# A decoder kernel whose softmax attentions mix the values over 8 or 16 columns a head instead of 128

## What is computed

```python
x = x + _L1_attn_ref(_layernorm(x), wq, wk, wv, wo)            # causal, 16 heads of 16
...
x = x + _L3_xattn_ref(_layernorm(x), ctx_1024, pos, pos, Wq, Wkv, Wout, bout)

def _L3_xattn_ref(x, ctx, ...):                                 # 32 heads of 8
    ...
    logits = jnp.einsum('bqhd,bkhd->bhqk', q, k) * scale
    w = jax.nn.softmax(logits, axis=-1)
    attn = jnp.einsum('bhqk,bkhd->bqhd', w, v)                  # the mixing of the values
    attn = attn.reshape(b, n, N_HEADS * HEAD_DIM)
    return attn @ Wout + bout
```

## Time and profile before

| | us |
|---|---|
| median of 3 runs | 2254.9 |
| lowest and highest | 2252.02, 2262.86 |
| span of the profiled execution | 2252.8 |
| TensorE matmul, weight load busy in it | 1368.1, 911.5 |
| VectorE, ScalarE, GpSimd busy in it | 1396.6, 559.6, 606.4 |

### The profile page before, as it was taken

The page is one execution under the profiler, slowest core; times in us unless marked ns, Lnnn a source line. Parts: engine busy times, 40 slices in busy tenths (PEclk is TensorE's granted clock), DMA queues, the critical chain, the costliest instruction groups (busy, mean ns, idle before and its releaser), DMA issues. The chain is left out here.

```text
span 2252.8 us, 24830 instructions
## 1 busy us (share of the span) xinstructions
PE 1368.1 (61%) x6308; PEld 911.5 (40%) x6308; DVE 1396.6 (62%) x2114; ACT 559.6 (25%) x1431; POOL 606.4 (27%) x449
## 2 busy tenths in 40 slices
PE   4525554887068943553597504798476989936760
PEld 2201123665038811111354303575244878825550
DVE  5489986333347758998875794312366767674332
ACT  1322211221016551220211001332124545502220
POOL 0046633332610005662200262133300000014335
PEclk8756665999579965656798756899687989968895
DMA  5112204986313021221000001207205310056773
GB/s 181 68 41 93 96 3 130 272 249 209 94 50 109 25 77 56 93 74 56 0 0 0 2 10 25 76 26 225 73 0 102 40 31 1 2 189 176 216 215 99
DMA packets 148450, 196.40 MB, mean 87 GB/s; under 512 B 34344, under 2 KB 109242, under 8 KB 147724
## 3 DMA queue, kind: packets, MB, share of 16 engines
q1 hardware_dynamic: 116876, 146.05, 21.8%
q0 software_dynamic: 11328, 30.95, 5.1%
q10 hardware_dynamic: 20160, 18.36, 2.4%
HBM read 153.55 MB, written 41.75 MB: 87 GB/s over the span
## 5 line engine op out<-in xcount | busy, mean ns | idle before, releaser
L141 POOL TENSOR_SCALAR rstd<-moments 128x8 f32<-128x8 f32 x12 | 2.9, 239 | 626.8 <-DVE moments L129 626.8
L442 PE MATMUL psum<-l1s_conv_out,w_ident 128*128 128x512 f32 x128 | 104.8, 965 | 107.6 <-DVE l1s_conv_out L538 107.6
L442 PE MATMUL psum<-l0s_conv_out,w_ident 128*128 128x512 f32 x128 | 103.0, 950 | 110.4 <-DVE l0s_conv_out L538 110.4
L1326 ACT ACTIVATE l3x_prob<-psum,l3x_neg_max 128x256 f32<-128x256 f32 x256 | 118.8, 469 | 107.4 <-DVE l3x_neg_max L1347 107.4
L534 DVE TENSOR_TENSOR_SCAN l1s_relu<-l1s_t_sq,l1s_xpad 128x1024 f32<-128x1024 f32 x32 | 139.7, 4365 | 5.2 <-ACT l1s_t_sq L505 5.2
L534 DVE TENSOR_TENSOR_SCAN l0s_relu<-l0s_t_sq,l0s_xpad 128x1024 f32<-128x1024 f32 x32 | 139.6, 4364 | 5.2 <-ACT l0s_t_sq L505 5.2
L1302 PE MATMUL psum<-l3x_v,l3x_probT 128*128 x1024 | 138.6, 279 | 1.1 <-DVE l3x_probT L1361 1.1
L152 PE MATMUL psum<-w_ident,h 128*128 128x128 f32 x144 | 32.4, 417 | 175.1 <-DVE h L133 175.1
L1347 DVE TENSOR_REDUCE l3x_neg_max<-psum 128x2 f32<-128x512 f32 x128 | 88.0, 690 | 67.2 <-PE psum L1267 67.2
L1302 PEld LDWEIGHTS psum<-l3x_v,l3x_probT 128*128 128x128 f32 x1024 | 127.5, 196 | 1.8 <-issue 1.8
L408 POOL TENSOR_TENSOR l1s_xpad<-l1s_du,l1s_bc 128x1024 f32<-128x1024 f32 x32 | 106.2, 3319 | 67.0 <-DVE l1s_relu L534 66.8
(11 more groups left out here) (577 smaller groups left out, 3498.1 us busy)
## 6 DMA issues: line engine op xcount, KB each, us to landing
l0f_w_in<-in_l0f_w_in SPq DMA_DIRECT2D x56, 352.0 KB
l0s_bc<-l0s_scratch SPq DMA_DIRECT2D x16, 1024.0 KB, 5.0
l1s_bc<-l1s_scratch SPq DMA_DIRECT2D x16, 1024.0 KB, 5.2
l3f_w_in<-in_l3f_w_in SPq DMA_DIRECT2D x64, 192.0 KB
l0f_w_down<-in_l0f_w_down SPq DMA_DIRECT2D x56, 176.0 KB
l2f_w_in<-in_l2f_w_in SPq DMA_DIRECT2D x24, 352.0 KB
l3f_y_rows<-h SPq DMA_DIRECT2D x16, 512.0 KB, 7.2
l3f_y_rows<-l3f_y ACTq DMA_DIRECT2D x64, 128.0 KB
```

The lines of the kernel that those rows point to most:

```text
L442: ins = nc.tensor.matmul(m.pair(2 + c)[:, cols], lhsT=m.ident[:], rhs=rhs[:, cols], start=start, stop=stop, skip_group_check=True)
L1326: ins = nc.scalar.activation(self.prob[h % self.SCORES][:, qt, 0:keys], self.bank(h % self.SCORES)[:, qt * S:qt * S + keys], ACT.Exp, bias ...
```

## The change

`mix` streams `self.hd` columns (16 in `l1a`, 8 in `l3x`) and writes as many. The stationary operand, the number and order of the instructions, the waits, the memory and its layout stay as they are.

```diff
--- before.py
+++ after.py
@@ -1297,9 +1297,9 @@
                 for qt in range(2):
                     kts = range(qt + 1) if self.causal else range(2)
                     for kt in kts:
-                        v = self.v[:, bass.ds(i * (2 * KD * 2 * P) + ((u * KD + c) * 2 + kt) * P + hh * self.hd, P)]
+                        v = self.v[:, bass.ds(i * (2 * KD * 2 * P) + ((u * KD + c) * 2 + kt) * P + hh * self.hd, self.hd)]
                         at = qt * 2 * P + hh * self.hd
-                        ins = nc.tensor.matmul(self.bank(6 + c)[:, at:at + P], lhsT=self.probT[h % 2][:, kt, qt, :],
+                        ins = nc.tensor.matmul(self.bank(6 + c)[:, at:at + self.hd], lhsT=self.probT[h % 2][:, kt, qt, :],
                                                rhs=v, start=(kt == 0), stop=(kt == kts[-1]))
                 ins.then_inc(self.mixed, 1)
```

## The result

The changed kernel takes 2469.7 us (median of 4 runs, 2464.3 to 2479.9) beside 2253.5 us for the kernel before (2248.2 to 2262.9): the ratio is 1.096, 95% interval 1.092 to 1.100. The forecast of 2479 us, slower, came out 9 us too high. The profiled execution has a span of 2478.0 us and lies 10 us above its median.

A forecast was written before the change was run, and what follows sets the result against it. TensorE was taken as the bound in `l3x`, with TensorE and VectorE both nearly full in `l1a`. Terms 64 + 156 + 4 = +224 on the 2252.8 us span gave 2477, 2479 as median; range 2405 to 2512.

The forecast's parts named there:

- The pace of a pass: L1302 in both loops: weight loads set the pace, so narrowing saves nothing; 0.111 us at high clock, 0.214 at low.
- The clock: `l1a` and `l3x`: streaming holds the clock, weight loads do not; both loops stay at 0.50 (1.2 GHz) in whole length.
- `l3x` loop: Context attention loop at the low clock throughout: 397 us where it had 241, +156; +180 with the seam unchanged.
- `l1a` loop: Causal attention loop at the low clock throughout: 156 us where it had 91.5, +64.
- the rest: Behind each loop, 16 transposes and the start of the projection at the low clock: about +2 each, +4.
- The seam of `l3x`: From mix to score: 0 to 0.1 us a unit saved at high clock; at low clock 0.15 us instead of 0.35.
- The middle of `l3x`: Waits mid-loop: 3.0 us ahead of the second trip, 2.9 for first exponentials, 1.5 for first copy; unchanged by slow clock.
- The seam of `l1a`: From mix to score: no seam, the score's load follows the mix with no rest; six passes 1.28 us.
- Only `l3x` stays low: Rival: `l1a` has more streaming left and rises in its first units; 2413 us, chance 0.10.
- The clock holds: Rival: in both loops scores and transposes alone lift the clock, only the seam is left; 0 to -12 us, chance 0.06.
- The clock goes up and down: Rival: in the loops, as in the state-space loop; half the term or less, 2300 to 2400 us, chance 0.04.
- The pace follows the columns: Rival: the mix costs next to nothing, VectorE bounds `l3x`, 50 us come off; about 2203 us, chance 0.02.

The follow-up runs named there:

- six wide units: Changed kernel, but the first six units of each trip of both loops stream 128 columns, all others 16 and 8: 2397.2 us, 1.062 of the kernel before.
- half-wide pair: Changed kernel with `l1a` at 128 columns, `l3x` matmuls alternating 128 and 8; from the first unit 2412.9 us, behind six fully wide units per trip 2245.3 us.
- half-wide behind six wide units: Changed kernel with `l1a` at 128 columns; `l3x` matmuls alternate 128 and 8 after six fully wide units per trip: 2245.3 us, 0.995 of the kernel before.

## Why the prediction was right

**The pace of a pass.** Held: 0.111 us with 16 or 8 columns at the high clock (run with six wide units), 0.214 at the low one (after). The forecast took the high one from L1602 and the routers and the low one from wide passes, and those rows carried over.

**The clock.** Held, with its place: both loops stay at 0.50 from their first unit to their last. The step "both loops begin at 0.50 and lose exactly what lifted them" was the right one, and the half-wide pair shows how much hangs on the first half of that sentence. One support of it was weak: "The one with 64 columns keeps 1.00" reads a hold from 3 us of a router. L1602 and the router with 16 columns, which fell, carried the argument.

**The Trainium skill's rule of idle gaps** ("TensorE: Matmul & The Clock Gate", section "Why this matters for your kernels": no idle gaps, and the clock stays up). In after, TensorE is busy 185.00 of 185.00 us at 0.50. The measurement decides against the rule for these loops.

**The Trainium skill's one rate for a weight load** ("TensorE: Matmul & The Clock Gate", section "LDWEIGHTS (loading the stationary operand)"). The page's formula, whatever the clock, gives an estimate of 107 ns for 128 columns. In the mixes of after one load follows another every 214 ns at 1.2 GHz; in the narrow mixes at 2.4 GHz (six wide units) it is 111 ns. The traces agree at the high clock only, and the +73 us that the page's figure gave are out.

**The terms.**

| term | forecast us | measured us |
|---|---|---|
| `l3x` loop | +156 | +162 |
| `l1a` loop | +64 | +53 |
| the rest | +4 | +10 |
| sum on the profiled spans | +224 | +225 |
| sum on the medians | | +216 |

That the sum on the spans is met within 1 us is luck: its terms miss by +6, -11 and +6 and cancel. On the medians the forecast is 8 us too high. The prediction also read the loops of before slightly too long: 1964.4 and 781.3 us are the starts of the last single load, so one load (0.2 us) had to be added and not a whole mix (0.97 and 0.7). That moves the two terms by less than 1 us each.

*The seam of `l3x`* was sized right: 1792.54 - 1790.68 = 1.86 us from the mix to the score at the low clock where 1.85 was forecast, and units of 3.09. *The middle of `l3x`* was not. Between the last transposes of the first trip and the first of the second 15.8 us pass in after and 9.4 in the kernel before. The slow passes of the last two mixes account for some 2 us of the difference; the forecast allowed for them, but not for the rest. In the profile of after, VectorE idles 8.8 us ahead of the first maximum of the second trip:

```profile
1973.76 1.46 PE L1267 MATMUL psum<-l3x_k_packed,l3x_q_packed 48*128 48x256 bf16 x6 [1.56 <-issue]
1974.38 5.74 SPq L1229 DMA_DIRECT2D l3x_k_packed<-l3x_parts  x6
1981.64 1.89 DVE L1347 TENSOR_REDUCE l3x_neg_max<-psum 128x2 f32<-128x512 f32 x3 [8.80 <-issue]
```

The scores are there by 1975.2 and no other engine releases it ("issue"), while SP's loads for the other sequence run. The extra 5 us are these. They do not need the low clock. The same time between the transposes is 11.7 to 13.8 us in the four other kernels whose `l3x` runs at 0.50 there, but of the kernels at the high clock three have 9.3 to 9.5 us (before, only `l1a` narrow, half-wide behind six wide units) and three have 11.3 to 13.6. In the one with only the last matmul narrow (13.6) VectorE idles 8.5 us by "issue" as well. What VectorE waits for there is not tested and stays open.

*The seam of `l1a`* is the term that was mis-sized. The prediction said "In `l1a` (96 rows) there is no such seam", and took the mix at 6 x 0.214 = 1.28 us, although its own row has 1.23 from the wide mix to the score (690.53 to 691.76). With a narrow last pass it is 699.70 - 698.56 = 1.14 us in after. At the high clock it is 0.58 (710.31 to 710.89, six wide units) instead of 0.67 (710.85 to 711.52, before). So narrowing lets the score in 0.09 us earlier at either clock, where the prediction put nothing. With 0.05 for the row that was not used, and a score of 0.60 instead of 0.64, a unit takes 2.27 us instead of 2.46: 0.19 less on 62 units, which is 11 us, the whole miss.

*The rest* is +10 in the profiled pair, of which the forecast's transposes and projections are at most 4. Of it 1.3 us lie ahead of the `l1a` loop, 0.4 between the loops and 8.6 behind `l3x`, where the last experts run: 297.0 us in after and 288.4 before. In the nine kernels of the experiments this stretch takes 288.7 to 293.8 us, whichever clock `l3x` had. As the profiled run lies 10 us above its median, and the medians differ by 216, I take the remainder as that execution's own; no run shows it.

**Rivals.** "Only `l3x` stays low" did not happen with 16 and 8 columns; it happened with 64. "The clock holds" did not happen either. With every pass of 16 columns `l1a` held it only behind wide units, and `l3x` fell even behind them; it kept the clock only where its opening was wide in at least three matmuls of four and at least one in four stayed wide behind it. "The clock goes up and down" shows nowhere in after; the nearest to it is one fall in each trip of `l3x` behind six wide units. "The pace follows the columns" has no support in any run.

## What to carry to other kernels

In a row of fp32 matmuls that each load a 128-column stationary operand, a pass took as long here with 8 moving columns as with 128 (0.111 us at 2.4 GHz, 0.214 at 1.2), so narrowing the moving side alone saved nothing but the tail of the last pass ahead of another kind of work, 0.10 us a unit in `l3x`. Before taking streaming out of a loop that is bound by TensorE, look at the granted clock at its start: the columns that seem wasted may be what lifts the clock. Such a loop can settle at either clock with the same instructions, and a few wide units at its start can decide which.

## What was not expected

- Either clock is kept to the end of a trip. Behind their openings, the same half-wide units of `l3x` ran at 3.09 us each in one kernel and at 1.70 in the other, a difference of 168 us that hangs on 12 units.
- A narrow last pass lets the next weight load start 0.09 us earlier even where no gap was to be seen between them (`l1a` at the low clock, 1.14 us instead of 1.23).
- Behind a wide opening, one wide matmul in four is enough to keep `l3x` at 2.4 GHz; with none it falls after three narrow units.
- The middle of `l3x` costs 9.3 to 15.8 us from kernel to kernel, long ones at either clock; why stays open.
